# Block numbers loaded singly, and k + e and v + e of a pair of steps in one instruction, in a graph transformer layer

## The chip, the cores and the metric

The kernel runs on one core of a Trainium2 chip. The metric is the device time of one execution in microseconds (us); of several executions the median counts. The engines are PE (TensorE), DVE (VectorE), ACT (ScalarE), POOL (GpSimd) and SP (SyncE, which only issues transfers). Each engine has a sequencer, which reads the instructions in order, waits for semaphores, handles registers and hands the work to the engine.

## The reference

One block of a graph network over 6250 nodes of 256 numbers and 106250 edges sorted by their target node: two graph attention layers (4 heads of 64), a linear attention over all nodes, and a mixture of 8 experts with top 2. All numbers are fp32. What the change touches is the edge part of a graph attention layer:

```python
q = (x @ Wq + bq).reshape(n, H, C); k = (x @ Wk + bk).reshape(n, H, C); v = (x @ Wv + bv).reshape(n, H, C)
e = (edge_attr @ We).reshape(-1, H, C)
kj = k[src] + e
vj = v[src] + e
logits = einsum('ehc,ehc->eh', q[dst], kj) / sqrt(C)
a = softmax of logits over the edges with the same dst
agg = segment_sum(vj * a[:, :, None], dst)
```

## The kernel before, in words

`build` runs one stage after the other: `plan`, `nodes` and `mix`, then for each of two layers `edges`, and after them `finish`, `route`, `dispatch`, `experts` and `combine`. The two `edges` stages are the long ones.

`edges` walks over 880 steps. A step is a tile of 128 edges together with the block of 128 target nodes that they go to; a tile that straddles two blocks makes two steps. `plan` writes two rows of numbers into `tab`, in partition 0 of SBUF: the tile of each step and, from column `z.NSP` on, its block. 20 steps (`T`) make a chunk, 10 (`HT`) a half, and there are 44 chunks. `chunks` writes out chunks 0 to 3, then runs a hardware loop of 20 iterations of two chunks (`p` is 0 in the first and 1 in the second), so 40 steps an iteration, and then writes out two more chunks that only finish lagging work. Every engine has such a loop of its own, and semaphores alone bring them into step.

For each step j of a chunk:

- SP loads the tile of edge attributes `ea`. POOL gathers k and v of the source nodes with an indirect transfer into `kv`, a ring of 10, and waits for `s_vj` before it fills a slot again.
- PE makes e = `ea` x `We` (L916, two halves, each in two passes) and q of the target nodes = `oht` x a block of `acc` (L919), both into `ps`, a ring of four PSUM banks. For L919 it needs the step's block number in a register. Then it makes `pa` (L938), the weighted sum of a step that lies 36 steps (`LAG`) back. L916 waits for `s_prod` of two pairs before, L938 for ACT's `w` and DVE's `s_acc`.
- DVE works on pairs of steps, `q` = 0 to 9 in a chunk, j = 2q. In a pair it adds `pa` of a lagging step into `acc` (L969, `add`), makes `kj` (L1016) and `vj` (L1028, a ring of 40 steps), adds the second lagging step (L969), multiplies `kj` by q (L1041) and reduces the product of the pair before (L977). Each `add` needs the block number of its lagging step in a register. Around the pairs stand a one-hot matrix for 10 steps (L961, twice a chunk) and short chains of small instructions for the maximum and its rescaling, at q = 2 to 5 and 8. Most of these small ones wait on `s_m` for the one before.
- ACT scales `vj` by the exponentials into `w` (L897, L899).

Block numbers go into registers through `table` (L102), which is one TENSOR_LOAD of the sequencer for up to 10 numbers. Before the change PE loads 10 at the start of each half, ahead of L916. DVE loads in an iteration 6 numbers at q = 0 of the first chunk, 10 at q = 3, 10 at q = 8 (its last ones are kept for the second chunk), and in the second chunk 10 at q = 3 and 4 at q = 8: five loads, 40 numbers.

Of the kernel before, what the change touches and what calls it, by code (L numbers as in the profile page):

```python
# [23 lines left out]
P = 128  # L24
D = 256
# [719 lines left out]
def edges(nc, z, g, layer, a):  # L745
# [3 lines left out]
    with Stage(nc, f"edge{layer}") as st:  # L749
# [7 lines left out]
        kj = st.sb("kj", [P, 2, 2, D])  # L757
        vj = st.sb("vj", [P, RV, D])
# [29 lines left out]
        s_we, s_np, s_far, s_oht, s_ix, s_step, s_spare, s_pe, s_kj, s_vj, s_prod, s_red = (  # L788
            st.sem(n) for n in ("s_we", "s_np", "s_far", "s_oht", "s_ix", "s_step", "s_spare", "s_pe", "s_kj", "s_vj", "s_prod", "s_red"))
# [16 lines left out]
        def main(c):  # L806
            return not isinstance(c, int) or c < NCH
# [95 lines left out]
        def _(pe):  # L903
# [3 lines left out]
            def chunk(c, p, u, kept):  # L907
                for j in range(T):
                    s = c * T + j
                    if main(c):  # L910
                        if j % HT == 0:
                            blocks = table(nc, pe, g.tab[0:1, bass.ds(z.NSP + s, HT)], z.NB - 1)
                        pe.wait_ge(s_ea[j % HT], 32 * c + 16 * (j // HT) + 16)
                        need(pe, s_prod, c * HT + j // 2 - 1)
                        for k in range(2):
                            nc.tensor.matmul(ps[:, j % 4, 0:D], ea[:, j % HT, k, :], We[:, k, :], start=(k == 0), stop=(k == 1))  # L916
                        if j % HT == 0:
                            pe.wait_ge(s_oht, 2 * c + j // HT + 1)
                        nc.tensor.matmul(ps[:, j % 4, D:2 * D], oht[:, j // HT, (j % HT) * P:(j % HT + 1) * P],  # L919
                                         g.q[:, bass.ds(blocks[j % HT], 1), 0:D].rearrange("p o d -> p (o d)"), start=True, stop=True).then_inc(s_pe, 1)  # L920
# [21 lines left out]
        def _(dve):  # L942
# [28 lines left out]

            def reduce(c, p, q):
# [7 lines left out]
            def chunk(c, p, u, kept):  # L980
# [8 lines left out]
                for q in range(HT):  # L989
# [4 lines left out]
                    if q == 0 and here is None and lagged(c, 0):  # L994
                        here = [None] * 4 + list(table(nc, dve, g.tab[0:1, bass.ds(z.NSP + c * T - LAG, 6)], z.NB - 1))
# [3 lines left out]
                    if q == 3 and lagged(c, j):  # L999
                        here = table(nc, dve, g.tab[0:1, bass.ds(z.NSP + c * T + j - LAG, HT)], z.NB - 1)  # L1000
                    if q == 8 and lagged(c, j):
                        here = table(nc, dve, g.tab[0:1, bass.ds(z.NSP + c * T + j - LAG, HT if not p and not isinstance(c, int) else 4)], z.NB - 1)
# [5 lines left out]
                    if lagged(c, j):  # L1008
                        if q == 8:
                            dve.wait_ge(s_resc, c)  # L1010
                        add(c, j, here[(j + 4) % HT])
                    if main(c):
# [3 lines left out]
                        nc.vector.tensor_tensor(kj[:, q % 2, :, :], kv[:, both, 0:D], e, ALU.add).then_inc(s_kj, 1)  # L1016
# [9 lines left out]
                    if main(c):  # L1026
                        need(dve, s_w, c * T + j - (RV - 2))
# [695 lines left out]
```

## Time and profile before

| what | us |
|---|---|
| median of 3 runs | 5624.68 (5619.65 to 5625.87) |
| the profiled execution, its own time | 5591.4 |
| its span, first to last instruction | 5589.5 |
| edges of layer 1, from its first L919 to its last add | 480.2 to 2402.5 |
| edges of layer 2, likewise | 2650.0 to 4593.3 |

The profile describes one execution. Its own time is 1.8 us more than its span, and 33 us (0.6%) under the median of the runs shown, so a difference found in the profile is taken off the median. The mean granted TensorE clock is 0.911; within the two loops of `edges` it is 0.95 and 0.96.

### The profile page before, as it was taken

The page shows a single profiled execution, that of the slowest core. Times are in us where ns is not written, and L with a number is a line of the kernel's source. Part 1 is how long each engine was busy: PE and PEld are TensorE (multiplying, and loading weights), DVE is VectorE, ACT ScalarE, POOL GpSimd, SP SyncE. Part 2 cuts the span into 40 slices and gives each one's busy share as a digit, 9 for nine tenths or more (in the row PEclk, how much of TensorE's full clock was granted, in tenths as well). Part 3 has the DMA queues.
Part 4 walks back from the last instruction along what each step waited for, and adds up shares of the span by engine and source line. Part 5 has one row for each costly group of instructions (what it writes and reads, how often), then busy time and mean ns, then how long its engine had stood idle before and what let it go on. Part 6 is the DMA issues. An engine that isn't in the chain of part 4 may idle for free. (4 is left out here: it accounts for less than half of the span.)

```text
span 5589.5 us, 99514 instructions
## 1 busy us (share of the span) xinstructions
PE 4402.2 (79%) x18414; PEld 3403.3 (61%) x18415; DVE 4000.3 (72%) x8475; ACT 2763.5 (49%) x10075; POOL 2149.0 (38%) x2298
## 2 busy tenths in 40 slices
PE   3977988888888888878988888888888873139980
PEld 1546777777777777633777777777777752126650
DVE  4446988888888888854988888888888877302222
ACT  0122666666666666631566666666666661013320
POOL 1013544444444444300544444444444424430005
PEclk9999999999999999989999999999999985569995
DMA  4468666666666666534866666666666633432225
GB/s 94 135 217 243 187 182 187 185 181 186 182 191 189 180 187 182 150 112 148 235 185 185 182 181 188 182 183 183 179 186 180 186 102 101 173 97 64 64 78 153
DMA packets 617069, 919.99 MB, mean 165 GB/s; under 512 B 114486, under 2 KB 478582, under 8 KB 616535
## 3 DMA queue, kind: packets, MB, share of 16 engines
q0 software_dynamic: 154544, 502.26, 31.6%
q1 hardware_dynamic: 378966, 326.18, 20.9%
q10 hardware_dynamic: 83280, 89.03, 4.6%
q14 instruction: 251, 2.05, 0.1%
q8 instruction: 28, 0.46, 0.0%
HBM read 803.82 MB, written 113.31 MB: 164 GB/s over the span
## 5 line engine op out<-in xcount | busy, mean ns | idle before, releaser
L859 POOL DMA_INDIRECT edge_kv<-kvD,edge_ix x1760 | 1812.2, 1030 | 1914.7 <-DVE edge_vj L1028 1612.1
L897 ACT ACTIVATE edge_w<-edge_vj,edge_ex 128x64 f32<-128x64 f32 x7040 | 1864.8, 337 | 1012.4 <-PE edge_pa L938 903.6
L916 PE MATMUL edge_ps<-edge_We,edge_ea 112*128 112x256 f32 x7040 | 1906.6, 394 | 201.2 <-issue 173.9
L916 PEld LDWEIGHTS edge_ps<-edge_We,edge_ea 112*128 112x128 f32 x7040 | 1363.4, 196 | 495.5 <-issue 252.8
L938 PE MATMUL edge_pa<-edge_w,edge_oh 128*128 128x260 f32 x3520 | 1143.9, 409 | 309.2 <-DVE acc L969 298.9
L969 DVE SCALAR_TENSOR_TENSOR acc<-acc,flag,edge_pa 128x260 f32 x1760 | 839.2, 477 | 411.8 <-issue 320.7
L919 PE MATMUL edge_ps<-acc,edge_oht 128*128 x3520 | 1089.7, 391 | 0.0
L938 PEld LDWEIGHTS edge_pa<-edge_w,edge_oh 128*128 128x128 f32 x3520 | 647.7, 198 | 523.5 <-issue 322.4
L919 PEld LDWEIGHTS edge_ps<-acc,edge_oht 128*128 128x128 f32 x3520 | 697.8, 198 | 104.5
L1016 DVE TENSOR_TENSOR edge_kj<-edge_kv,edge_ps 128x512 f32<-128x512 f32 x880 | 600.0, 682 | 118.0 <-PE edge_ps L919 114.6
L1041 DVE TENSOR_TENSOR edge_prod<-edge_kj,edge_ps 128x512 f32<-128x512 f32 x880 | 598.6, 680 | 0.0
L1028 DVE TENSOR_TENSOR edge_vj<-edge_kv,edge_ps 128x512 f32<-128x512 f32 x880 | 597.3, 679 | 0.0
L977 DVE TENSOR_REDUCE edge_Lc<-edge_prod 128x8 f32<-128x512 f32 x880 | 597.2, 679 | 0.0
L470 PE MATMUL nodes_pj<-nodes_W,nodes_xT 128*128 128x512 f32 x784 | 361.7, 606 | 28.1 <-ACT nodes_xT L411 28.1
L899 ACT ACTIVATE edge_w<-edge_ex 128x4 f32<-128x4 f32 x1760 | 343.2, 195 | 0.0
L872 ACT ACTIVATE edge_oht<-edge_kb,edge_npart 128x1280 f32<-128x1280 uint8 x178 | 239.9, 1348 | 198.6 <-POOLq L858 101.4
L1544 DVE TENSOR_TENSOR exp_hb<-exp_pH,b 128x512 f32<-128x512 f32 x108 | 74.7, 692 | 325.9 <-PE exp_pH L1487 325.9
L961 DVE TENSOR_TENSOR edge_oh<-free,relS 128x1280 f32<-128x1280 f32 x176 | 260.8, 1482 | 0.0
L470 PEld LDWEIGHTS nodes_pj<-nodes_W,nodes_xT 128*128 128x128 f32 x784 | 144.3, 194 | 182.5 <-issue 146.0
L874 ACT ACTIVATE edge_oht<-edge_oht,ones 128x1280 f32<-128x1280 f32 x178 | 242.5, 1362 | 5.8
L542 DVE TENSOR_TENSOR acc<-nodes_pj,nodes_bias 128x256 f32 (+1 forms) x98 | 41.6, 425 | 236.2 <-PE nodes_pj L470 236.2
L1487 PE MATMUL exp_pH<-W,exp_xT 128*128 x432 | 205.3, 598 | 0.1
(230 smaller groups left out, 2878.6 us busy)
## 6 DMA issues: line engine op xcount, KB each, us to landing
edge_ea<-ea_t_dram SPq DMA_DIRECT2D x1760, 112.0 KB, 3.5
edge_kb<-relD SPq DMA_DIRECT2D x178, 160.0 KB
edge_kv<-kvD,edge_ix POOLq DMA_INDIRECT x1760, 4.4
kvD<-nodes_kvs ACTq DMA_DIRECT2D x98, 256.0 KB
xsD<-mix_zr POOLq DMA_DIRECT2D x27, 512.0 KB
exp_xr<-xsD SPq DMA_DIRECT2D x108, 128.0 KB, 2.1
ysD<-exp_yo ACTq DMA_DIRECT2D x108, 128.0 KB, 1.7
edge_pen<-penD SPq DMA_DIRECT2D x352, 32.0 KB
```

Of the source, the lines that this page charges most:

```text
L470: ins = nc.tensor.matmul(pj[:, j % 2, n * 2 * D:(n + 1) * 2 * D], xT[:, j, c, :], W[:, c, n * 2 * D:(n + 1) * 2 * D], start=(c == 0), stop ...
L859: nc.gpsimd.indirect_dma_start(out=kv[:, j % HT, :], out_offset=None, in_=g.kvD, in_offset=bass.IndirectOffsetOnAxis(ap=ix[:, h, j % HT:j ...
L897: nc.scalar.activation(w[:, j % 4, h * CA:h * CA + C], vj[:, slot, h * C:(h + 1) * C], ACT.Copy, scale=ex[:, x, h, k:k + 1])
L899: nc.scalar.activation(w[:, j % 4, :].rearrange("p (h k) -> p h k", h=H)[:, :, C], ex[:, x, :, k], ACT.Copy).then_inc(s_w, 1)
L916: nc.tensor.matmul(ps[:, j % 4, 0:D], ea[:, j % HT, k, :], We[:, k, :], start=(k == 0), stop=(k == 1))
L919: nc.tensor.matmul(ps[:, j % 4, D:2 * D], oht[:, j // HT, (j % HT) * P:(j % HT + 1) * P], g.q[:, bass.ds(blocks[j % HT], 1), 0:D].rearrang ...
L938: nc.tensor.matmul(pa[:, j % 2, 0:A], oh[:, par, (j + 4) % HT, :], w[:, j % 4, :], start=True, stop=True).then_inc(s_ape, 1)
L969: nc.vector.scalar_tensor_tensor(out=at, in0=at, scalar=g.flag[:, bass.ds(n, 1)], in1=pa[:, j % 2, 0:A], op0=ALU.mult, op1=ALU.add).then_i ...
L977: nc.vector.tensor_reduce(Lc[:, p, :, s:s + 2].rearrange("p h s -> p s h"), prod[:, q % 2, :, :].rearrange("p s (h k) -> p s h k", h=H), A ...
L1016: nc.vector.tensor_tensor(kj[:, q % 2, :, :], kv[:, both, 0:D], e, ALU.add).then_inc(s_kj, 1)
L1028: nc.vector.tensor_tensor(vj[:, p * T + j:p * T + j + 2, :], kv[:, both, D:2 * D], e, ALU.add).then_inc(s_vj, 1)
L1041: nc.vector.tensor_tensor(prod[:, q % 2, :, :], kj[:, q % 2, :, :], ps[:, bank, D:2 * D], ALU.mult).then_inc(s_prod, 1)
```

## The change

PE no longer loads ten block numbers before L916 of a half; it loads one number in every step, between L916 and L919. DVE no longer loads up to ten numbers at a time ahead of the first `add`; it loads two in every pair, for the pair that follows, behind the instruction that makes k + e and v + e and ahead of the second `add`. That instruction is new: `kj` and `vj` lie in one tile `kvj`, four rows for kj and forty for vj, and one TENSOR_TENSOR of 1024 elements a partition writes both, reading e twice through a stride of zero. The semaphore `s_kj` falls away and `s_vj` serves for both.

```diff
-        kj = st.sb("kj", [P, 2, 2, D])
-        vj = st.sb("vj", [P, RV, D])
+        kvj = st.sb("kvj", [P, 4 + RV, D])
+        vj = kvj[:, 4:4 + RV, :]
...
-                        if j % HT == 0:
-                            blocks = table(nc, pe, g.tab[0:1, bass.ds(z.NSP + s, HT)], z.NB - 1)
...
+                        block = table(nc, pe, g.tab[0:1, bass.ds(z.NSP + s, 1)], z.NB - 1)[0]
...
+            def both_of(row, slot):
+
+                at = kvj[:, row:row + 2, :]
+                part, pair, el = at.ap
+                return bass.AP(at.tensor, at.offset, [part, pair, [(4 + slot - row) * D, 2], el])
+
+            def blocks(n):
+                return table(nc, dve, g.tab[0:1, bass.ds(z.NSP + n, 2)], z.NB - 1)
...
-                    if q == 0 and here is None and lagged(c, 0):
-                        here = [None] * 4 + list(table(nc, dve, g.tab[0:1, bass.ds(z.NSP + c * T - LAG, 6)], z.NB - 1))
+                    if here is None and lagged(c, j):
+                        here = blocks(c * T + j - LAG)
...
-                    if q == 3 and lagged(c, j):
-                        here = table(nc, dve, g.tab[0:1, bass.ds(z.NSP + c * T + j - LAG, HT)], z.NB - 1)
...
-                        nc.vector.tensor_tensor(kj[:, q % 2, :, :], kv[:, both, 0:D], e, ALU.add).then_inc(s_kj, 1)
+                        need(dve, s_w, c * T + j - (RV - 2))
+                        nc.vector.tensor_tensor(both_of(2 * (q % 2), p * T + j), kv[:, both, :].rearrange("p t (b d) -> p t b d", b=2),
+                                                e.unsqueeze(2).to_broadcast([P, 2, 2, D]), ALU.add).then_inc(s_vj, 1)
...
-                    if main(c):
-                        need(dve, s_w, c * T + j - (RV - 2))
-                        nc.vector.tensor_tensor(vj[:, p * T + j:p * T + j + 2, :], kv[:, both, D:2 * D], e, ALU.add).then_inc(s_vj, 1)
                     if q == 5 and closed(c):
                         step(12)
                         nc.vector.tensor_scalar(Ym[:, :], mask4[:, :], dl[:, 0:1], None, ALU.mult).then_inc(s_Y, 1)
+                    if q == HT - 1 and (p or isinstance(c, int)):
+                        then = None
+                    elif lagged(c, j + 2):
+                        then = blocks(c * T + j + 2 - LAG)
+                    else:
+                        then = None
...
-                        add(c, j + 1, here[(j + 5) % HT])
+                        add(c, j + 1, here[1])
+                    here = then
```

**DVE at q = 3 of a chunk in the loop.** L102 ISA and TENSOR_LOAD are the register load; L969 (L968 in the changed file) is the add. Before:

```order
L998 STREAM_TRANSPOSE edge_TT<-edge_FB 128x32
L102 ISA
L102 TENSOR_LOAD tab
L966 REGISTER_ALU
L969 ISA
L969 SCALAR_TENSOR_TENSOR acc<-acc,flag,edge_pa 128x260
L1015 REGISTER_ALU
L1016 TENSOR_TENSOR edge_kj<-edge_kv,edge_ps 128x512
L986 REGISTER_ALU
L1024 SCALAR_TENSOR_TENSOR edge_X<-edge_wp,edge_R,edge_TT 128x20
L1025 SCALAR_TENSOR_TENSOR edge_Y<-edge_wp,edge_TT 128x20
L1028 TENSOR_TENSOR edge_vj<-edge_kv,edge_ps 128x512
```

After the change the same place reads:

```order
L1006 STREAM_TRANSPOSE edge_TT<-edge_FB 128x32
L965 REGISTER_ALU
L968 ISA
L968 SCALAR_TENSOR_TENSOR acc<-acc,flag,edge_pa 128x260
L1019 REGISTER_ALU
L1021 TENSOR_TENSOR edge_kvj<-edge_kv,edge_ps 128x2x2x256
L994 REGISTER_ALU
L1030 SCALAR_TENSOR_TENSOR edge_X<-edge_wp,edge_R,edge_TT 128x20
L1031 SCALAR_TENSOR_TENSOR edge_Y<-edge_wp,edge_TT 128x20
L102 ISA
L102 TENSOR_LOAD tab
L994 REGISTER_ALU
```

The load has moved from between the transposition and the first add to behind the large instruction, and it is of two numbers. The copy of R (L1034, then L1043), which waits for both scans, follows the load, with no vj between it and the scans.

**DVE at q = 5.** Before, vj stood between dl (L1020) and Ym (L1031), which waits for dl. After the change:

```order
L1021 TENSOR_TENSOR edge_kvj<-edge_kv,edge_ps 128x2x2x256
L994 REGISTER_ALU
L1025 TENSOR_TENSOR edge_Df<-edge_pm,edge_B 128x128
L1026 SCALAR_TENSOR_TENSOR edge_dl<-edge_GX,edge_B 128x1
L994 REGISTER_ALU
L1034 TENSOR_SCALAR edge_Ym<-edge_mask,edge_dl 128x4
L102 ISA
L102 TENSOR_LOAD tab
L965 REGISTER_ALU
L968 ISA
L968 SCALAR_TENSOR_TENSOR acc<-acc,flag,edge_pa 128x260
```

Ym stands directly behind dl, and the register load directly behind Ym.

**PE, a step inside a half** (L916 is L914 in the changed file, L919 is L918, L938 is L937). Before:

```order
L916 MATMUL edge_ps<-edge_We,edge_ea 128x256 x2
L919 ISA
L919 MATMUL edge_ps<-acc,edge_oht 128x256
L935 REGISTER_ALU
L938 MATMUL edge_pa<-edge_w,edge_oh 128x260
```

After:

```order
L914 MATMUL edge_ps<-edge_We,edge_ea 128x256 x2
L102 ISA
L102 TENSOR_LOAD tab
L918 ISA
L918 MATMUL edge_ps<-acc,edge_oht 128x256
L934 REGISTER_ALU
L937 MATMUL edge_pa<-edge_w,edge_oh 128x260
```

A register load of one number stands in each step between the two kinds of matmul, and the load of ten at the head of a half is gone.

## Rows read from the trace of the kernel before

**Rows 1.** The page: busy time of each engine, share of the span, instructions.

```profile
PE 4402.2 (79%) x18414; PEld 3403.3 (61%) x18415; DVE 4000.3 (72%) x8475; ACT 2763.5 (49%) x10075; POOL 2149.0 (38%) x2298
```

**Rows 2.** DVE's loop branches: count, ns min/median/max, first and last start; layer 1, then 2.

```profile
L800 DVEq COMPARE_BRANCH  x20: 60/68/74, 708.6 to 2361.4; - x20
...
L800 DVEq COMPARE_BRANCH  x20: 55/63/74, 2880.3 to 4552.0; - x20
```

**Rows 3.** DVE's waits, 708.6 to 2361.4: us in total, times, longest.

```profile
DVE acc L969 <- issue: 134.8, 52, 3.1
DVE edge_kj L1016 <- PE edge_ps L919: 37.6, 63, 1.9
DVE acc L969 <- PE edge_pa L938: 26.0, 20, 2.4
```

**Rows 4.** DVE's timeline in pairs 0 to 2: start us, duration us.

```profile
1505.03 1.48 DVE L961 TENSOR_TENSOR edge_oh<-free,relS 128x1280 f32<-128x1280 f32 x1
1506.43 0.48 DVE L969 SCALAR_TENSOR_TENSOR acc<-acc,flag,edge_pa 128x260 f32 x1
...
1509.61 0.47 DVE L969 SCALAR_TENSOR_TENSOR acc<-acc,flag,edge_pa 128x260 f32 x1
1510.01 0.68 DVE L1016 TENSOR_TENSOR edge_kj<-edge_kv,edge_ps 128x512 f32<-128x512 f32 x1
1510.60 0.68 DVE L1028 TENSOR_TENSOR edge_vj<-edge_kv,edge_ps 128x512 f32<-128x512 f32 x1
1511.20 0.48 DVE L969 SCALAR_TENSOR_TENSOR acc<-acc,flag,edge_pa 128x260 f32 x1
```

**Rows 5.** DVE's timeline at q = 3 of the same chunk; idle time in brackets.

```profile
1513.54 0.21 DVE L998 STREAM_TRANSPOSE edge_TT<-edge_FB 128x32 f32<-128x32 f32 x1
1516.27 0.48 DVE L969 SCALAR_TENSOR_TENSOR acc<-acc,flag,edge_pa 128x260 f32 x1 [2.52 <-issue]
```

**Rows 6.** Register loads of one iteration, L102: ns min/median/max, start us.

```profile
L102 DVEq TENSOR_LOAD <-tab x1: 837/837/837, 1500.7 to 1500.7; - x1
...
L102 DVEq TENSOR_LOAD <-tab x1: 2291/2291/2291, 1513.7 to 1513.7; - x1
...
L102 DVEq TENSOR_LOAD <-tab x1: 1061/1061/1061, 1534.1 to 1534.1; - x1
...
L102 DVEq TENSOR_LOAD <-tab x1: 349/349/349, 1575.9 to 1575.9; - x1
...
L102 PEldq TENSOR_LOAD <-tab x1: 2402/2402/2402, 1519.1 to 1519.1; - x1
```

**Rows 7.** DVE's timeline around the load at q = 8.

```profile
1533.31 0.68 DVE L1016 TENSOR_TENSOR edge_kj<-edge_kv,edge_ps 128x512 f32<-128x512 f32 x1
...
1536.10 0.42 DVE L1007 TENSOR_TENSOR acc<-acc,edge_fn 128x260 f32 x1
```

**Rows 8.** PE's register loads in `experts`, one number each.

```profile
L1471 PEldq TENSOR_LOAD <-etab x216: 297/302/546, 4977.7 to 5420.3; - x108
```

**Rows 9.** DVE around a loop branch: sequencer's records, then its timeline.

```profile
L800 DVEq COMPARE_BRANCH  x1: 68/68/68, 1497.1 to 1497.1; - x1
L800 DVEq FUSED_REGOPS  x1: 98/98/98, 1500.5 to 1500.5; - x1
...
1501.85 0.48 DVE L969 SCALAR_TENSOR_TENSOR acc<-acc,flag,edge_pa 128x260 f32 x1 [2.70 <-issue]
```

**Rows 10.** dl and Ym with nothing between them, behind the loop.

```profile
2378.08 0.21 DVE L1020 SCALAR_TENSOR_TENSOR edge_dl<-edge_GX,edge_B 128x1 f32<-128x1 f32 x1
2378.33 0.23 DVE L1031 TENSOR_SCALAR edge_Ym<-edge_mask,edge_dl 128x4 f32<-128x4 f32 x1
```

**Rows 11.** PE's timeline: two steps, and the one behind its load of ten.

```profile
1509.42 1.03 PE L916 MATMUL edge_ps<-edge_We,edge_ea 112*128 112x256 f32 x4
...
1511.16 1.03 PE L916 MATMUL edge_ps<-edge_We,edge_ea 112*128 112x256 f32 x4
...
1521.75 1.13 PE L916 MATMUL edge_ps<-edge_We,edge_ea 112*128 112x256 f32 x4 [1.12 <-issue]
```

More of the change, by code:

```diff
@@ L787, in edges @@
         s_pen = [st.sem(f"s_pen{h}") for h in range(2)]
-        s_we, s_np, s_far, s_oht, s_ix, s_step, s_spare, s_pe, s_kj, s_vj, s_prod, s_red = (
-            st.sem(n) for n in ("s_we", "s_np", "s_far", "s_oht", "s_ix", "s_step", "s_spare", "s_pe", "s_kj", "s_vj", "s_prod", "s_red"))
+        s_we, s_np, s_far, s_oht, s_ix, s_step, s_spare, s_pe, s_vj, s_prod, s_red = (
+            st.sem(n) for n in ("s_we", "s_np", "s_far", "s_oht", "s_ix", "s_step", "s_spare", "s_pe", "s_vj", "s_prod", "s_red"))
         s_oh, s_w, s_ape, s_acc, s_init = (st.sem(n) for n in ("s_oh", "s_w", "s_ape", "s_acc", "s_init"))
@@ L919, in chunk @@
                         nc.tensor.matmul(ps[:, j % 4, D:2 * D], oht[:, j // HT, (j % HT) * P:(j % HT + 1) * P],
-                                         g.q[:, bass.ds(blocks[j % HT], 1), 0:D].rearrange("p o d -> p (o d)"), start=True, stop=True).then_inc(s_pe, 1)
+                                         g.q[:, bass.ds(block, 1), 0:D].rearrange("p o d -> p (o d)"), start=True, stop=True).then_inc(s_pe, 1)
                     if closed(c):
@@ L998, in chunk @@
                         nc.vector.transpose(TT[:, :], FB[:, 112:144]).then_inc(s_m, 1)
-                    if q == 3 and lagged(c, j):
-                        here = table(nc, dve, g.tab[0:1, bass.ds(z.NSP + c * T + j - LAG, HT)], z.NB - 1)
-                    if q == 8 and lagged(c, j):
-                        here = table(nc, dve, g.tab[0:1, bass.ds(z.NSP + c * T + j - LAG, HT if not p and not isinstance(c, int) else 4)], z.NB - 1)
                     if q == 8 and closed(c):
@@ L1010, in chunk @@
                             dve.wait_ge(s_resc, c)
-                        add(c, j, here[(j + 4) % HT])
+                        add(c, j, here[0])
                     if main(c):
@@ L1037, in chunk @@
                     if lagged(c, j + 1):
[L1038 removed]
+                        add(c, j + 1, here[1])
+                    here = then
                     if main(c):
[L1040 to L1041 removed]
+                        dve.wait_ge(s_vj, c * HT + q + 1)
+                        nc.vector.tensor_tensor(prod[:, q % 2, :, :], kvj[:, 2 * (q % 2):2 * (q % 2) + 2, :], ps[:, bank, D:2 * D], ALU.mult).then_inc(s_prod, 1)
                     if q == 4 and closed(c):
```

2 lines of the change are left out of this document (removed).

## The prediction

> **What bounds the kernel now.** I read the page first. PE has the larger busy share, 79% to DVE's 72% [rows 1], which says little, since other stages are in it. The loops of `edges` are where the change acts, so I took DVE's loop branches next: 19 intervals in 1652.8 us of layer 1 and in 1671.7 us of layer 2 [rows 2], 87.0 and 88.0 us an iteration of 40 steps. 40 iterations at 87.5 are 3500 us of 5589.
>
> In them PE repeats a step every 1.74 us where nothing holds it (1509.42 to 1511.16 [rows 11]), 69.6 us for 40 steps, about 71.5 with the small matmuls. That leaves it 16 us of slack. DVE has less. Its waits in layer 1 [rows 3], divided by 19, are 7.1 us for "issue", 2.0 us for PE's L919 and 1.4 us for PE's L938, some 10.5 in all; the remaining 76.5 it works. So DVE sets the pace, and what shortens DVE's own stream or its stalls comes off the time, until 71.5 is reached.
>
> An issue stall is DVE's sequencer reading registers. At q = 3 the transposition starts at 1513.54 and the next add at 1516.27, 2.52 us idle [rows 5], and the load of ten lasts from 1513.7 for 2.29 us [rows 6]. At q = 8 a load of ten begins at 1534.1 [rows 6], just when kj, which the product before it waits for, has ended (1533.31 + 0.68), and L1007 starts at 1536.10 with no idle time [rows 7]. The sequencer had handed out four instructions and loaded beneath them. So a load costs nothing where work is queued ahead of it, and everything where the sequencer has just waited for DVE's newest result.
>
> **Cost of a load.** The durations [rows 6] are 2.29 us for ten numbers at q = 3, 1.06 for ten at q = 8, 0.84 for six, 0.35 for four; PE takes 2.40 for ten, and 0.30 for a single one [rows 8]. The fast ones start at a column divisible by four (20c - 20, 20c - 36), the slow ones two beyond (20c - 30, 20c + 10). It fits that four aligned numbers are read at once and all others singly, at 0.30 for the first and 0.22 to 0.24 for each further. A load of two is then 0.30 + 0.24 = 0.54 us; the bounds are 0.30 (read together) and 0.84 (the load of six).
>
> **The change part by part, for an iteration.**
>
> Removed: the two stalls at q = 3, 2 x 2.52 = 5.0 us. The loads at q = 8 were hidden, so nothing comes back there.
>
> Merged: kj and vj start 0.59 and 0.60 us apart from what follows, 1.19 us for both, and 1280 elements take 1.40 (1505.03 to 1506.43) [rows 4]. From 512 to 1280 elements that is 1.05 ns an element, so 1024 take 1.13 us: 0.06 less a pair, 1.2 us for 20 pairs. L961 reads both inputs by broadcast and keeps that rate, so I take the same for a zero stride; it reads no PSUM, and the other bound is no gain at all, 0.0.
>
> The Trainium skill ("VectorE: DVE Perf Modes", section on the TRN2 errata) puts a fixed 120 cycles on each PSUM source instruction, 125 ns. By it the merge would give 2.5 us an iteration instead of 1.2, and the sum would be about 50 us lower. The trace's 0.595 us for 512 elements leaves only 0.06 us of fixed part, and I go by the trace.
>
> PE's loads: the stall of 1.12 us at 1521.75 [rows 11] is the rest of its load of 2.40. The load of one (0.30), its address (0.05) and the way from a load's end to a started matmul (1521.5 to 1521.75, 0.25) make 0.60 us a step. Above them lie the four passes of L916 just handed out, 1.03 us [rows 11]. I cost them at nothing; without the cover they would be 24 us an iteration. Of DVE's 2.0 us of waits for L919, which follow PE's stalls, I take 1.5 as gone.
>
> The Trainium skill ("DMA: Bandwidth & Descriptors", section "Latency and other measured facts") gives a register load a floor of about 600 ns, to be spread by unrolling, which speaks against loading singly. By it PE's chain would be 0.90 us, still under 1.03, and the forecast would move by some 5 us only. The 216 single loads at 0.302 us contradict it.
>
> DVE's loads in an ordinary pair: the sequencer passes the product's wait when the large instruction ends, hands out product and reduction, waits for the add before (done about 0.1 us later), hands out the next add and the next large instruction, and loads for 0.6 us. The engine needs 0.40 + 0.60 + 0.60 + 0.40 + 1.13 = 3.1 us for what is queued. Cost nothing; uncovered it would be 0.85 us, as follows.
>
> Added at q = 5: Ym must wait for dl with nothing between, 0.25 us from start to start [rows 10] where 0.13 is usual for so small an instruction, so 0.12. Then the load starts about 0.16 after Ym (1513.54 to 1513.7 at q = 3), lasts 0.54, and the add starts 0.27 after its end (1516.0 to 1516.27). These 0.97 less Ym's own 0.22 are 0.75. Together 0.9, twice an iteration 1.8 us.
>
> Added at q = 3: the copy of R directly behind the scans, about 0.1, twice 0.2 us. The load there lies beneath the large instruction, handed out just before.
>
> The loop branch: DVE's sequencer takes 3.4 us from branch to first instruction (1497.1 to 1500.5), then loads six numbers, and 2.70 us show as idle [rows 9]. Queued above it were vj, add, product and reduction. After the change vj is not among them (0.6 us less cover), and the load is 0.3 us shorter: 0.3 us more.
>
> Sum: -5.0 - 1.2 - 1.5 + 1.8 + 0.2 + 0.3 = -5.4 us an iteration, -216 us for 40. The four written-out chunks with both kinds of work (2 and 3 in each layer) lose about 2.6 each, -10; in chunks 0 and 1, which PE limits, some of its eight load stalls go, an estimate of -9. Total -235 us. The profiled execution's 5591.4 becomes 5356; the median of 5624.68, from which I take the same difference, 5390.
>
> **The rivals.**
>
> *Part of the gain is missing.* The merged instruction saves nothing (+48 us), or PE, which needs 3.48 us a pair against DVE's 3.1, holds DVE up in the stretches with no extra DVE work, so that its 2.0 us of waits stay (+60). For it: 63 waits on L919, 0.6 us in the mean, stand in 19 iterations now [rows 3]. Against: the one-hot's 1.40 us and the chains give PE its lead back twice a chunk. Both together make 5498; one of them 5440 to 5450.
>
> *More is gained.* Waits for L938 and the longer issue stalls (up to 3.1 us [rows 3]) shrink as well since PE no longer stands: up to 2 us more an iteration, 5310.
>
> *Slower: PE's single loads are not hidden.* The place is between L916 and L919 in each step. If PE's sequencer cannot reach the load while L916 runs, 0.60 us a step turn 71.5 into 95.5 us an iteration, 8 above today: 40 x 8 = +320, about 5945. It decides when more than 16 / 40 = 0.40 us a step is exposed. Against it: PE's load of ten began at 1519.1 and cost only 1.12 us of idle, so it ran beneath matmuls [rows 6, 11].
>
> *DVE's loads are not hidden.* 18 pairs an iteration at 0.85 us would be 15 us more, a net +10, and 6015; it would be slower than before from 0.30 us a load. The hidden load of ten at q = 8 speaks against it. So does the one of four.
>
> *No change.* DVE's gains are eaten by another wait, such as ACT's or the gathers'. POOL is busy for 38% and ACT for 49% [rows 1], so I find none.
>
> **How the numbers follow.** The forecast's case, 5340 to 5430, has 0.67. Part of the gain missing (5430 to 5530) has 0.16, more gained (under 5340) 0.07, no change 0.03, slower by either way 0.07. The range of 8 in 10 runs from 5335 to 5480; it holds either of the smaller losses but not both. 0.2% of the time, 11 us, is about what a measurement of this kernel tells from no change. Faster 0.90, same 0.03, slower 0.07.
>
> **What would show it.** The interval of DVE's branches falls from 87.0 and 88.0 to about 82. L102 on DVE shows 0.54 us for two numbers, on PE 0.30 for one. The idle 2.52 us before L969 at q = 3 is gone, and about 0.75 appears before the second add at q = 5. The large instruction's duration is 1.22 us, and the next starts 1.13 after it. PE shows no idle time between L914 and L918. The prediction is wrong if the ordinary pair takes over 3.2 us, if PE's step exceeds 2.0 us, or if idle time appears before adds in every pair.

## The result, and the profile after

The changed kernel takes 5324.68 us in the median of 4 runs (5321.81 to 5326.23), the kernel before 5625.27 in the 4 runs beside it: a ratio of 0.9458, 95% interval 0.9432 to 0.9484. That is 300 us less, where 235 were forecast, and 10 us below the range. The profiled execution took 5325.0 us, its span 5322.8.

The page, to be held against [rows 1]: busy time of each engine.

```profile
PE 4324.0 (81%) x18414; PEld 3332.1 (63%) x18415; DVE 3957.8 (74%) x7595; ACT 2772.1 (52%) x10075; POOL 2076.2 (39%) x2298
```

DVE's loop branches in layer 1 and layer 2, as [rows 2]:

```profile
L800 DVEq COMPARE_BRANCH  x20: 55/63/74, 710.1 to 2242.8; - x20
...
L800 DVEq COMPARE_BRANCH  x20: 55/63/74, 2762.1 to 4292.4; - x20
```

Nineteen intervals each: 80.67 and 80.54 us for 40 steps, where [rows 2] gave 87.0 and 88.0. So the loops give 6.3 and 7.4 us an iteration, and the forecast said 5.4.

The waits of DVE between the first and last of those branches of layer 1, as [rows 3] (us in total, times, the longest):

```profile
DVE acc L968 <- issue: 89.0, 57, 3.8
DVE acc L968 <- DVE acc L1011: 11.4, 38, 0.3
DVE edge_kvj L1021 <- PE edge_ps L918: 2.2, 1, 2.2
...
DVE acc L968 <- PE edge_pa L937: 0.2, 1, 0.2
```

The two waits for PE, 63 and 20 times in [rows 3], have come down to one each. "Issue" falls from 134.8 us to 89.0; its 57 times are three an iteration, the two at q = 5 and the branch. The wait behind L1011 (L1007 before), 11.4 us, is the same in the kernel before. Layer 2, between its first and last of those branches, first before (2880.3 to 4552.0), then after (2762.1 to 4292.4):

```profile
DVE acc L969 <- issue: 161.9, 57, 3.8
DVE edge_kj L1016 <- PE edge_ps L919: 41.5, 64, 1.9
DVE acc L969 <- PE edge_pa L938: 13.9, 18, 1.7
```

```profile
DVE acc L968 <- issue: 86.2, 57, 3.6
...
DVE edge_kvj L1021 <- PE edge_ps L918: 2.9, 2, 2.3
```

The register loads (ns min/median/max), as [rows 6, 8]:

```profile
L102 PEldq TENSOR_LOAD <-tab x1760: 295/302/494, 480.5 to 4288.4; - x196
...
L102 DVEq TENSOR_LOAD <-tab x880: 522/528/778, 545.9 to 4326.4; - x176
```

DVE in order of time (start, duration, idle time before it). An iteration's q = 5, with an ordinary pair behind it, as [rows 4]:

```profile
1502.26 0.21 DVE L1026 SCALAR_TENSOR_TENSOR edge_dl<-edge_GX,edge_B 128x1 f32<-128x1 f32 x1
1502.51 0.23 DVE L1034 TENSOR_SCALAR edge_Ym<-edge_mask,edge_dl 128x4 f32<-128x4 f32 x1
1503.48 0.48 DVE L968 SCALAR_TENSOR_TENSOR acc<-acc,flag,edge_pa 128x260 f32 x1 [0.74 <-issue]
...
1506.87 1.21 DVE L1021 TENSOR_TENSOR edge_kvj<-edge_kv,edge_ps 128x1024 f32<-128x1024 f32 x1
1508.00 0.48 DVE L968 SCALAR_TENSOR_TENSOR acc<-acc,flag,edge_pa 128x260 f32 x1
...
1509.98 1.22 DVE L1021 TENSOR_TENSOR edge_kvj<-edge_kv,edge_ps 128x1024 f32<-128x1024 f32 x1
```

The large instruction holds the engine for 1.13 us (1506.87 to 1508.00), the pair lasts 3.11 (to the next large one at 1509.98). The load of two stands under the large instruction and the add, and nothing is idle. At q = 5 nothing is queued above the load but small instructions: 0.74 us. The loop branch and q = 3, as [rows 9, 5]:

```profile
1522.80 0.49 DVE L968 SCALAR_TENSOR_TENSOR acc<-acc,flag,edge_pa 128x260 f32 x1 [3.07 <-issue]
...
1534.31 0.21 DVE L1006 STREAM_TRANSPOSE edge_TT<-edge_FB 128x32 f32<-128x32 f32 x1
1534.61 0.48 DVE L968 SCALAR_TENSOR_TENSOR acc<-acc,flag,edge_pa 128x260 f32 x1
```

The 2.52 us of q = 3 are gone. The branch shows 3.07 instead of 2.70.

### The profile page after: what moved, and what is told of

It is laid out like the page before. It is cut to its first block and busy times, and to the rows that moved or that the text cites. A ratio compares the mean times of both kernels' runs of the same rounds, so it can differ in the third digit from the quotient of the medians.

```text
span 5322.8 us, 103674 instructions
## 1 busy us (share of the span) xinstructions
PE 4324.0 (81%) x18414; PEld 3332.1 (63%) x18415; DVE 3957.8 (74%) x7595; ACT 2772.1 (52%) x10075; POOL 2076.2 (39%) x2298
## 5 line engine op out<-in xcount | busy, mean ns | idle before, releaser
L859 POOL DMA_INDIRECT edge_kv<-kvD,edge_ix x1760 | 1737.6, 987 | 1726.0 <-DVE edge_kvj L1021 1152.7
L897 ACT ACTIVATE edge_w<-edge_kvj,edge_ex 128x64 f32<-128x64 f32 x7040 | 1865.3, 337 | 838.4 <-PE edge_pa L937 576.2
L914 PE MATMUL edge_ps<-edge_We,edge_ea 112*128 112x256 f32 x7040 | 1855.1, 386 | 45.0 <-DVE edge_prod L1051 23.2
L914 PEld LDWEIGHTS edge_ps<-edge_We,edge_ea 112*128 112x128 f32 x7040 | 1334.3, 192 | 291.7 <-issue 88.7
L937 PE MATMUL edge_pa<-edge_w,edge_oh 128*128 128x260 f32 x3520 | 1119.1, 401 | 281.8 <-DVE acc L968 174.9
L1021 DVE TENSOR_TENSOR edge_kvj<-edge_kv,edge_ps 128x1024 f32<-128x1024 f32 x880 | 1068.6, 1214 | 58.5 <-PE edge_ps L918 28.7
L918 PE MATMUL edge_ps<-acc,edge_oht 128*128 x3520 | 1063.5, 383 | 0.0
L968 DVE SCALAR_TENSOR_TENSOR acc<-acc,flag,edge_pa 128x260 f32 x1760 | 842.0, 478 | 235.8 <-issue 180.6
L937 PEld LDWEIGHTS edge_pa<-edge_w,edge_oh 128*128 128x128 f32 x3520 | 615.2, 191 | 534.1 <-ACT edge_w L899 249.6
L918 PEld LDWEIGHTS edge_ps<-acc,edge_oht 128*128 128x128 f32 x3520 | 679.9, 193 | 96.8
L1051 DVE TENSOR_TENSOR edge_prod<-edge_kvj,edge_ps 128x512 f32<-128x512 f32 x880 | 599.1, 681 | 1.1
L1515 PE MATMUL exp_pY<-W,exp_hT 128*128 x864 | 204.3, 379 | 0.0
```

The lines of the kernel that those rows point to most:

```text
L859: nc.gpsimd.indirect_dma_start(out=kv[:, j % HT, :], out_offset=None, in_=g.kvD, in_offset=bass.IndirectOffsetOnAxis(ap=ix[:, h, j % HT:j ...
L897: nc.scalar.activation(w[:, j % 4, h * CA:h * CA + C], vj[:, slot, h * C:(h + 1) * C], ACT.Copy, scale=ex[:, x, h, k:k + 1])
L937: nc.tensor.matmul(pa[:, j % 2, 0:A], oh[:, par, (j + 4) % HT, :], w[:, j % 4, :], start=True, stop=True).then_inc(s_ape, 1)
L968: nc.vector.scalar_tensor_tensor(out=at, in0=at, scalar=g.flag[:, bass.ds(n, 1)], in1=pa[:, j % 2, 0:A], op0=ALU.mult, op1=ALU.add).then_i ...
L1021: nc.vector.tensor_tensor(both_of(2 * (q % 2), p * T + j), kv[:, both, :].rearrange("p t (b d) -> p t b d", b=2), e.unsqueeze(2).to_broadc ...
L1051: nc.vector.tensor_tensor(prod[:, q % 2, :, :], kvj[:, 2 * (q % 2):2 * (q % 2) + 2, :], ps[:, bank, D:2 * D], ALU.mult).then_inc(s_prod, 1)
```

## The experiments

Medians of two kernels that were not run side by side are compared by their ratio to the kernel before, which ran beside each. Interval means DVE's loop interval, nineteen of them in each layer (nine of 80 steps, halved, in the last three rows with the long loop).

| kernel | median us | ratio, 95% interval | interval in layer 1, 2 |
|---|---|---|---|
| e1 before again | 5617.6 | 1.0005 (0.9985 to 1.0024) | 87.9, 87.5 |
| e2 merge only | 5652.1 | 1.0072 (1.0049 to 1.0095) | 87.8, 88.6 |
| e3 DVE's loads only | 5467.9 | 0.9741 (0.9719 to 0.9763) | 84.1, 83.5 |
| e4 PE's loads only | 5482.4 | 0.9769 (0.9747 to 0.9791) | 83.8, 85.0 |
| e5 both loads, no merge | 5259.8 | 0.9390 (0.9363 to 0.9417) | 79.5, 79.5 |
| e6 merge and DVE's loads | 5512.4 | 0.9847 (0.9821 to 0.9873) | 85.7, 85.5 |
| the change, all three | 5324.7 | 0.9458 (0.9432 to 0.9484) | 80.7, 80.5 |
| e7 the change, loads at the large instruction | 5224.5 | 0.9330 (0.9303 to 0.9357) | 79.0, 78.9 |
| e8 before, aligned loads | 5331.9 | 0.9512 (0.9485 to 0.9540) | 80.6, 81.4 |
| e9 the change, q = 5 load moved | 5233.0 | 0.9337 (0.9312 to 0.9363) | 79.1, 79.1 |
| e10 the change, four chunks a loop | 5318.3 | 0.9496 (0.9469 to 0.9522) | 79.7, 82.3 |
| e11 e7, four chunks a loop | 5258.9 | 0.9381 (0.9355 to 0.9407) | 78.3, 81.2 |
| e12 e7, four chunks for DVE alone | 5189.8 | 0.9260 (0.9242 to 0.9277) | 77.6, 77.7 |

**e1: the kernel before, unchanged.** 

> The kernel before, unchanged, for a second trace of it. The profiled execution of before was 5591, its medians 5625, while the changed kernel's executions all lie within 5 us. Theory 1 (the offset is real and sits in the loops): this trace shows a loop interval of DVE above 87.5 us in both layers, the 3.4 us from branch to first instruction nearer to the 4.0 that layer 2 had, and a time near 5625. Theory 2 (the first profile was an odd one in other stages): the loop intervals are again 87.0 and 88.0, and the difference lies outside the loops.

The profiled execution of before had been 33 us under its medians; this one has a span of 5625.1. Its loops differ from those of the first trace by +17 us in layer 1 and -9 in layer 2; the rest, 28 us, lies outside the loops: 13 ahead of the first branch of layer 1 and 14 between the two layers' loops. So the trace of before that the prediction used was a short one (the 12 executions here lie between 5589 and 5636), and mostly outside the loops. DVE's waits over its nineteen iterations of layer 1 (722.0 to 2392.1):

```profile
DVE acc L969 <- issue: 148.9, 89, 3.0
DVE edge_kj L1016 <- PE edge_ps L919: 43.0, 53, 2.0
DVE acc L969 <- PE edge_pa L938: 29.8, 22, 2.4
```

**e2: the merged instruction alone,** block numbers loaded as before.

```diff
-                        nc.vector.tensor_tensor(kj[:, q % 2, :, :], kv[:, both, 0:D], e, ALU.add).then_inc(s_kj, 1)
+                        nc.vector.tensor_tensor(both_of(2 * (q % 2), p * T + j), kv[:, both, :].rearrange("p t (b d) -> p t b d", b=2),
+                                                e.unsqueeze(2).to_broadcast([P, 2, 2, D]), ALU.add).then_inc(s_vj, 1)
...
-                        nc.vector.tensor_tensor(vj[:, p * T + j:p * T + j + 2, :], kv[:, both, D:2 * D], e, ALU.add).then_inc(s_vj, 1)
```

> Before, with k + e and v + e in one instruction and all register loads as before. My theory (sizes as predicted): 0.06 us a pair saved, 1.2 us an iteration, against 0.4 for Ym and R directly behind what they wait for and up to 0.6 less cover at the loop branch: -0.2 us an iteration, about 5615, not clearly different from before. Rival (the merge carries a good part of the 300 us): 1.2 us or more an iteration, 5570 or less.

It made the kernel slower, by 0.5 to 1.0%, where no clear difference was expected. Its waits in 710 to 2240:

```profile
DVE acc L969 <- issue: 152.0, 60, 3.8
DVE edge_kvj L1023 <- PE edge_ps L919: 30.9, 28, 2.2
DVE acc L969 <- PE edge_pa L938: 12.3, 13, 1.7
DVE edge_kvj L1023 <- issue: 11.0, 23, 0.7
```

In e1 the same stretch has 136.6 us of issue before L969 and 2.4 before L1016, and 39.9 and 29.8 of waits for PE. So 24 us more of sequencer time show here, in 17.4 iterations, which fits that vj no longer stands as cover between a load or a branch and the add; 26 us less of waits for PE go against it, as a DVE that is late waits less. What the merge saves is spent on that, and in layer 2, whose interval is 1.1 us longer than e1's, more than that.

**e3: DVE's loads alone,** two numbers in every pair, PE and the two instructions as before.

```diff
-                        here = table(nc, dve, g.tab[0:1, bass.ds(z.NSP + c * T + j - LAG, HT)], z.NB - 1)
...
+                        then = blocks(c * T + j + 2 - LAG)
```

> Before, with DVE's block numbers loaded in pairs, kj and vj apart, PE loading ten as before. My theory: the two idle stretches of 2.5 us at q = 3 go, little comes at q = 5 since vj stands before Ym, and 0.3 goes at the branch: -5.3 us an iteration, about 5400. Rival (PE's load of ten then becomes what holds the pairs, since both engines stall near each other): PE waits rise above 3 us an iteration and the time stays above 5450.

```profile
DVE acc L969 <- PE edge_pa L938: 50.8, 48, 2.3
DVE edge_kj L1015 <- PE edge_ps L919: 43.4, 43, 1.9
DVE acc L969 <- issue: 34.0, 37, 2.4
```

In 710 to 2240, 18.2 iterations: issue before the add has fallen from 7.8 us an iteration to 1.9, but the waits for PE stand at 5.2 (e1: 4.0 in the same stretch). A DVE that stalls less waits for PE more, and the interval falls by 3.9 instead of 6. So the rival of the expectation came true, with waits above 3 us and a time over 5450.

**e4: PE's single loads alone.**

```diff
-                        if j % HT == 0:
-                            blocks = table(nc, pe, g.tab[0:1, bass.ds(z.NSP + s, HT)], z.NB - 1)
...
+                        block = table(nc, pe, g.tab[0:1, bass.ds(z.NSP + s, 1)], z.NB - 1)[0]
```

> Before, with PE's block number loaded singly and DVE as before. My theory: the waits of DVE for L919, 2.0 us an iteration, go almost wholly: -1.5 to -2.5 us, 5525 to 5565. Rival 1 (single loads are exposed on PE): slower than before. Rival 2 (the waits for L919 come from elsewhere): no change, 5615 to 5625.

```profile
DVE acc L968 <- issue: 142.6, 66, 2.9
...
DVE edge_kj L1015 <- PE edge_ps L918: 2.6, 4, 2.0
```

This is the run that decides. With nothing changed but PE's loads, 69.7 us of waits for PE (39.9 for L919 and 29.8 for L938 in e1's 710 to 2240) are 2.6, and L938's do not appear at all. In layer 2 (e1 2924.7 to 4587.0, e4 2824.6 to 4439.2) 47.7 us are 9.0. The interval falls by 4.1 us in layer 1 and 2.5 in layer 2, 3.3 in the mean where 1.5 to 2.5 were expected, and the time by 2.3%.

TensorE's clock is a rival that this run bears on. In the trace of before the clock fell for a few microseconds twice in the iteration of [rows 4], each time behind some 2.5 us in which PE had waited for DVE's add: the granted clock was 0.60 in 1517 to 1521 and 0.72 in 1557 to 1561, so most of the first stretch ran at the lower of its two levels (1.2 and 2.4 GHz). A PE at half speed could have made DVE wait just as well. But e4's clock is hardly higher (0.97 in 710 to 2190 and 0.96 in 2770 to 4190, where e1 has 0.95 and 0.96), and DVE hardly waits for PE. So these stretches alone do not hold DVE up; how much they add to a stall of PE's load, no run shows.

**e5: both kinds of load, kj and vj apart.** 

> The changed kernel without the merge: DVE loads in pairs, PE singly, kj and vj apart. Theory 1 (the merge's 1.2 us an iteration is paid back, since with kj and vj apart nothing stands exposed at q = 5 and 0.6 us more work covers the loop branch): DVE idle about 3 us an iteration, interval about 79, 5260 to 5300, faster than the changed kernel. Theory 2 (the merge brings its 1.2 us once the loads are right): 5365 to 5380.

DVE's waits over its nineteen iterations of layer 1 (697.7 to 2208.6), and the three of one iteration in order of time, two at q = 5 and the one behind the branch:

```profile
DVE acc L968 <- issue: 59.1, 57, 3.0
```

```profile
1520.14 0.48 DVE L968 SCALAR_TENSOR_TENSOR acc<-acc,flag,edge_pa 128x260 f32 x1 [0.29 <-issue]
1558.94 0.48 DVE L968 SCALAR_TENSOR_TENSOR acc<-acc,flag,edge_pa 128x260 f32 x1 [0.63 <-issue]
1577.66 0.48 DVE L968 SCALAR_TENSOR_TENSOR acc<-acc,flag,edge_pa 128x260 f32 x1 [2.21 <-issue]
```

No wait for PE is left. It is faster than the whole change: 0.7% by the ratios, 38 us, and 1.1 us an iteration, 44 us, by the loops. (By the medians it is 65, but the kernel before ran 23 us shorter beside e5 to e8 than beside the changed kernel.) vj still stands between dl and Ym, and that shortens the idle time at q = 5 without taking it away: 0.29 and 0.63 us where the changed kernel has 0.74 twice. Behind the branch it is 2.21 where the changed kernel has 3.07. Together 3.1 us an iteration are idle here and 4.7 there. Apart, e3 and e4 gave 147 and 133 us, 280 together; here it is 343, so DVE's gain by its own loads is paid out in full only when PE is not late.

**e6: the merge with DVE's loads, PE as before.** 

> The changed kernel with PE's loads of ten as before. Theory 1 (PE's loads of ten hold DVE up by 3.9 us an iteration whatever DVE does): 5460 to 5480. Theory 2 (PE's part matters only beside DVE's own stalls, which are gone here): 60 us or less above the changed kernel, 5385 or less.

```profile
DVE acc L969 <- PE edge_pa L938: 72.1, 68, 1.8
DVE acc L969 <- issue: 50.6, 17, 3.5
DVE edge_kvj L1022 <- PE edge_ps L919: 47.4, 54, 1.9
```

119.5 us of waits for PE in 17.9 iterations, 6.7 each: the most of all kernels. The time, 5512, is above both theories'. Without PE's part the other two are worth 90 us of 300.

**e7: the change, with DVE's load of two directly behind the large instruction,** ahead of the chains, in every pair.

```diff
                                                 e.unsqueeze(2).to_broadcast([P, 2, 2, D]), ALU.add).then_inc(s_vj, 1)
+                    if q == HT - 1 and (p or isinstance(c, int)):
+                        then = None
+                    elif lagged(c, j + 2):
+                        then = blocks(c * T + j + 2 - LAG)
+                    else:
+                        then = None
                     if q == 5 and closed(c):
```

> The changed kernel with the pair's register load directly behind the large instruction at every q, so ahead of Df, dl and Ym at q = 5. If the 0.74 us of idle at q = 5 are the load alone: idle gone, 1.5 us an iteration, 60 us, about 5265. Rival (Ym's wait for dl is the stall, wherever the load stands): 5315 to 5325.

```profile
1468.99 0.23 DVE L1040 TENSOR_SCALAR edge_Ym<-edge_mask,edge_dl 128x4 f32<-128x4 f32 x1
1469.28 0.48 DVE L968 SCALAR_TENSOR_TENSOR acc<-acc,flag,edge_pa 128x260 f32 x1
```

The 0.74 us before the add at q = 5 are gone, twice an iteration, and the interval falls by 1.6 to 1.7: 66 us for 40. By the ratios (0.9330 against 0.9458) the gain is 72 us. The two profiled spans differ by 99; the other 33 lie outside the loops (the first branch stands at 694.9 instead of 710.1, and 495.0 us lie between the layers' loops instead of 519.3), of the size by which two executions of the kernel before differ there, too (e1). But e9 has most of it again (697.3 and 501.2), so it need not be spread; its cause is open. Against e5, the kernel without the merge, this one is 0.5 us an iteration faster. That does not show the merge to be worth anything: e5 still has its load behind vj and Ym and 0.9 us of idle time at q = 5 in layer 1, 0.6 in layer 2. An estimate from these numbers puts e5 with its load moved at 79.5 - 0.9 = 78.6 and 79.5 - 0.6 = 78.9 us, no slower than the 79.0 and 78.9 here; no run tried it.

**e8: the kernel before with its loads of ten made loads of twelve that start two numbers earlier,** at a column divisible by four. PE's loads of ten at the head of a chunk (j = 0) already start at such a column; they keep their start and are made twelve long. Only the loads change; the two extra numbers are not used.

```diff
-                            blocks = table(nc, pe, g.tab[0:1, bass.ds(z.NSP + s, HT)], z.NB - 1)
+                            blocks = table(nc, pe, g.tab[0:1, bass.ds(z.NSP + s - (2 if j else 0), HT + 2)], z.NB - 1)[(2 if j else 0):]
...
-                        here = table(nc, dve, g.tab[0:1, bass.ds(z.NSP + c * T + j - LAG, HT)], z.NB - 1)
+                        here = table(nc, dve, g.tab[0:1, bass.ds(z.NSP + c * T + j - LAG - 2, HT + 2)], z.NB - 1)[2:]
```

> The kernel before, with the two kinds of slow loads starting two numbers earlier, at a column divisible by four, and reading twelve numbers of which the first two are left unused. If four aligned numbers are read at once: 0.8 us instead of 2.3 to 2.4 on DVE and PE, idle time at q = 3 falls by 1.5 us and the waits for PE by most of 4, together 5 to 6 us an iteration, 5380 to 5430. If each number costs 0.23 wherever it lies: 2.8 us a load, and about 5640.

Its loads in 1400 to 1600, and the stall at q = 3:

```profile
L102 DVEq TENSOR_LOAD <-tab x13: 352/853/1074, 1401.4 to 1591.3; - x13
...
L102 PEldq TENSOR_LOAD <-tab x10: 846/850/854, 1405.5 to 1586.3; - x10
```

```profile
1524.76 0.48 DVE L969 SCALAR_TENSOR_TENSOR acc<-acc,flag,edge_pa 128x260 f32 x1 [1.08 <-issue]
```

Twelve numbers in 0.85 us where ten took 2.29 and 2.40 (and 1.09 on PE at j = 0). The stall falls from 2.52 to 1.08, DVE has no wait for PE left in 710 to 2240, and the old kernel with its loads aligned has 90% of the change's gain (0.9512 against 0.9458). The time is 48 us below the expected range.

**e9: the change, with only the load of q = 5 moved** behind the large instruction.

```diff
+                    if q == 5:
+                        then = blocks(c * T + j + 2 - LAG) if lagged(c, j + 2) else None
```

> The changed kernel with one load moved: at q = 5 alone DVE's two numbers are loaded directly behind the large instruction, before the chain of dl and Ym; at every other q the load stays where the change put it. In e7, where all were moved, the loops gained 1.6 us an iteration (64 us for 40) and the stretches outside the loops another 35 to 40. Theory 1: the uncovered load at q = 5 is the whole of what the loops gained, two of 0.74 us an iteration: loop interval about 79.0 us, and 60 us less than the changed kernel, about 5265. The gain outside the loops then does not come with it (or, if it does, the same uncovered load also stretched the written-out chunks: then 5225). Theory 2: the place of the load matters in every pair, since behind the large instruction it is covered by more: then this kernel keeps part of the 80.6 us interval, 79.8 or more, and comes out over 5290.

In 775 to 2195, 18 iterations, DVE's issue waits are 55.6 us in 18 times, one an iteration, that of the branch. The loop intervals are e7's within 0.12 us and the ratio lies within e7's interval: in the loops the load at q = 5 was all of it, and in the other pairs its place does not matter. The time is 32 us under the 5265 of the theory, by what lies outside the loops (e7).

**e10: the change, with the hardware loop written out for four chunks,** 10 iterations of 80 steps.

```diff
-            with eng.Fori(2, NCH // 2) as i:
-                kept = chunk(2 * i, 0, i, None)
-                chunk(2 * i + 1, 1, i, kept)
+            with eng.Fori(1, NCH // 4) as i:
+                for k in range(2):
+                    kept = chunk(4 * i + 2 * k, 0, 2 * i + k, None)
+                    chunk(4 * i + 2 * k + 1, 1, 2 * i + k, kept)
```

> The changed kernel with the hardware loop written out for four chunks an iteration instead of two, so 10 iterations instead of 20 in a layer and 20 loop branches fewer in all on each engine. Theory 1: DVE's sequencer shows about 3.1 us idle before the first add behind each branch, and within an iteration the same place costs next to nothing, so 20 x 3 = 60 us go: about 5265. Theory 2: the time behind the branch is taken up by the slack of the other engines (PE waits in its turn for DVE, and its own branch lies in the same place), so half or less is gained, 5295 or more. Theory 3: the longer loop body costs instruction fetches elsewhere, no gain: 5320.

**e11: e7 with the same loop.** 

> The kernel of e7 (all of DVE's loads directly behind the large instruction) with the hardware loop of four chunks. If the two costs are separate, the gains add: 5224 less what e10 shows, 5165 if that is 60. If PE becomes the bound once DVE's idle time is gone (its step is 1.74 us where nothing holds it, 69.6 us for 40 steps and some 71.5 with the small matmuls, against an interval of 79 now), less is gained, but with 7 us of slack an iteration that is not expected: over 5200 would say so.

Neither paid: e10's interval of the ratio overlaps the change's, and e11 is 0.5% slower than e7 (e7's five executions lie between 5222 and 5234 us, e11's between 5251 and 5266). In layer 1 both loops are faster, by 1.0 and 0.7 us for 40 steps, in layer 2 slower, by 1.8 and 2.3. The branches in layer 2 (2700 to 4150; ns min/median/max), first e7's, then e11's:

```profile
L800 ACTq COMPARE_BRANCH  x18: 45/45/45, 2760.8 to 4102.6; - x18
L800 ACTq FUSED_REGOPS  x18: 59/59/59, 2761.0 to 4102.9; - x18
L800 PEldq COMPARE_BRANCH  x18: 207/208/208, 2766.8 to 4108.7; - x18
```

```profile
L800 ACTq COMPARE_BRANCH  x9: 45/45/45, 2758.9 to 4057.8; - x9
L800 ACTq FUSED_REGOPS  x9: 59/59/64, 2761.8 to 4060.3; - x9
L800 PEldq COMPARE_BRANCH  x9: 5206/5304/5620, 2765.0 to 4063.9; - x9
...
L800 DVEq COMPARE_BRANCH  x9: 63/63/74, 2767.6 to 4066.5; - x9
L800 DVEq FUSED_REGOPS  x9: 98/98/104, 2771.3 to 4070.4; - x9
```

From the branch to the instruction behind it (FUSED_REGOPS) ACT takes 0.2 us in the short loop and 2.5 to 2.9 in the long one; PE's branch itself takes 0.21 and 5.3 (3.8 in layer 1); DVE takes 3.7 to 3.9 in the long loop and 3.5 to 3.6 in e7's (its first here from 2769.4 to 2773.0). The transfers of instructions bear on what PE does there. e11's queue q8 of them in 2767.6 to 4229.5, nine iterations (transfers, MB, share of the DMA engines):

```profile
q8 instruction: 89, 1.46, 0.5%
```

In e7's eighteen iterations (2769.4 to 4190.3) and in e12, where DVE's loop alone is long, q8 carries nothing. PE in e11, behind such a branch:

```profile
3095.87 1.05 PE L915 MATMUL edge_ps<-edge_We,edge_ea 112*128 112x256 f32 x2 [5.01 <-issue]
3100.28 1.01 PE L915 MATMUL edge_ps<-edge_We,edge_ea 112*128 112x256 f32 x2 [3.35 <-issue]
...
3102.88 1.91 PE L915 MATMUL edge_ps<-edge_We,edge_ea 112*128 112x256 f32 x4
```

PE stands for 5.0 and 3.35 us, and DVE waits 77.4 us for L938 in 2770 to 4190, nine times (e7: none). Two of q8's transfers start right behind the branch (in 3090 to 3093) and a third, of 2.1 us, at 3096.7, where the second idle stretch begins. That fits a PE that waits there for its next instructions, but no run tests it. After the idle time PE's clock is at its lower level: the four passes of L915 take 1.91 us at a granted clock of 0.50 (3102.8 to 3104.8), where they take 1.03 at full clock. Over 2770 to 4190 the granted clock is 0.97 instead of e7's 0.99.

**e12: e7 with the loop of four chunks for DVE alone.**

```diff
+            if after == 3:
+                with eng.Fori(1, NCH // 4) as i:
...
+            else:
+                with eng.Fori(2, NCH // 2) as i:
...
-            chunks(dve, chunk)
+            chunks(dve, chunk, 3)
```

> The kernel of e7, with the loop of four chunks for DVE alone; PE, ACT, POOL and SP keep the loop of two. In e11, where all have the long loop, PE's COMPARE_BRANCH takes 3.7 us (layer 1) and 5.5 us (layer 2) instead of 0.21, and ACT's next instruction stands 2.6 us behind its branch instead of 0.2. Theory 1: those longer fetches of PE (two idle stretches of 5.0 and 3.35 us for each branch in layer 2) ate what DVE saved. With PE's loop short again DVE keeps 10 uncovered branches of about 3 us less in each layer: 77.4 to 77.7 us for 40 steps in both layers, 5160 to 5180. Theory 2: DVE's time behind a branch grows with its loop as PE's does (3.4 us in e7; 6 or more here), so that half as many cost as much: 5210 to 5230. Theory 3: DVE is held up by something else as soon as it runs faster, such as POOL's gathers: waits for L918 or for the transfer of kv appear, 5190 to 5220.

DVE's waits in 775 to 2160:

```profile
DVE acc L974 <- issue: 29.5, 9, 3.6
```

The intervals are theory 1's, 77.6 and 77.7 us, in both layers. The time is 10 us above theory 1's and at the edge of theory 3's, but none of theory 3's waits shows in layer 1, and 2.3 us of one for PE's L943 in layer 2 (2770 to 4150); the rest lies outside the loops again (581.1 us from layer 1's last branch to layer 2's first, at 2754.6; to the same step they are 573.9 in e7). It is the fastest kernel of the study, 7.4% under the kernel before and 2.1% under the changed one by their ratios.

## Why the prediction was wrong

The direction, the mechanism and the steps of DVE's own stream were right; one term of the sum was taken too small. The table sets the sum against the trace of before that it was made from and against e1's, over the loops of both layers (38 iterations), in us an iteration:

| term | predicted | before | after | after less before | after less e1 |
|---|---|---|---|---|---|
| sequencer idle (issue): q = 3 gone, q = 5 and branch added | -5.0 + 1.5 + 0.3 = -3.2 | 7.81 | 4.61 | -3.20 | -3.67 |
| waits for PE's L919 (after: L918) | -1.5 | 2.08 | 0.13 | -1.95 | -1.99 |
| waits for PE's L938 (after: L937) | 0 | 1.05 | 0.02 | -1.03 | -1.03 |
| add behind L1007 (after: L1011), q = 8 | 0 | 0.60 | 0.60 | 0 | +0.39 |
| work of DVE: merge, and the chain's gaps at q = 5 and 3 | -1.2 + 0.3 + 0.2 = -0.7 | | | -0.70, the rest | -0.79 |
| interval | -5.4 | 87.49 | 80.61 | -6.88 | -7.09 |

(e1's waits in layer 2, 2924.7 to 4587.0: 165.7 us of issue, 37.8 for L919, 9.9 for L938, 4.2 behind L1007; the last is 3.6 in layer 1.)

- **Waits for PE (the step that failed).** "Of DVE's 2.0 us of waits for L919, which follow PE's stalls, I take 1.5 as gone": all of them went, and so did L938's, which the sum left in. It was to be -3.0 and stood as -1.5. The 1.5 us missing are 60 us for 40 iterations, and the miss is 66 (300 us against 235); what is left is within what two executions differ by. e4 shows it without any change to DVE, and there the removal of PE's stalls is worth 3.3 us an iteration. In layer 1 alone the waits for L938 were larger (1.4 us, and 0.7 in layer 2).
- The error was to hold PE innocent because it had 16 us of slack an iteration. The slack is a mean. What the traces fit is that a stall of PE at the start of a half meets DVE at a place where PE has no lead, and nobody pays DVE back for a wait. The rival "more is gained" named this, at 5310, with a chance of 0.07 that was too low: nothing in [rows 3] spoke for L938's waits staying.
- **Cost of a load.** Predicted 0.54 us for two and 0.30 for one; measured 0.528 and 0.302. That the start of a load decides is confirmed by e8. But the rule as the prediction words it, four aligned numbers at once and all others singly, does not give the slow loads: ten numbers that start two beyond a multiple of four hold two aligned groups of four, and by it would take about as long as the 1.06 us of ten that start aligned. They took 2.29, as ten single ones would. What fits all the loads is that fours are counted from the start of the load and go at once only where that start is aligned; why is open. The Trainium skill ("DMA: Bandwidth & Descriptors", section "Latency and other measured facts") has a floor of about 600 ns for a register load; the trace does not agree, 1760 loads of PE have a median of 0.302 us.
- **q = 3, q = 5, the branch, the ordinary pair.** Predicted: 2.52 gone, 0.75 added before the second add, the branch 0.3 longer, no idle time in an ordinary pair of 3.1. Measured: gone, 0.74, 3.07 for 2.70, 3.11.
- **The merge.** Predicted 0.06 us less a pair; the engine is held for 1.13 us, as forecast, where two instructions took 1.19 [rows 4]. The term was right, but it was not the merge's whole effect: a part of the 1.8 us at q = 5 and the 0.3 at the branch, which the sum adds elsewhere, are also the merge's, since it takes vj away as cover (e5, with vj there, has 0.9 us of idle time at q = 5 and 0.9 less behind the branch). The sum had the pieces to say that the merge is a loss with the loads in this place, and did not say it. e5 against the change shows 38 us, e2 against e1 about 35.
- **The 125 ns rule.** The Trainium skill ("VectorE: DVE Perf Modes", section on the TRN2 errata) puts a fixed 120 cycles on each instruction that reads PSUM. One such instruction fewer a pair saved 0.06 us from start to start and not 0.125: as a saving of time the trace does not agree. The durations do: 0.68 us for 512 elements and 1.21 for 1024, where estimates by the page's formula are 0.66 and 1.19. But the next instruction starts 0.08 us before the end of the one ahead, and so only a part of the fixed cost counts.
- **PE's single loads hidden.** Right: PE's step stays at 1.74 us (L914 at 1507.61, 1509.35, 1511.08), and the rival that they show is out.
- **Outside the loops** -19 us were forecast. The spans of e1 and after differ by 302, the loops by 7.1 x 40 = 284 when the 38 intervals' mean stands for all 40, which leaves 18. From the trace of before the spans differ by 267, the loops by 6.9 x 40 = 275, and outside them after is 8 us longer. Two executions differ by more than this term, which stays unproven.

The forecast took the profile's difference off the median. From e1's trace the spans differ by 302 us, as the medians do (300); from the trace of before, which was short outside the loops, by 267. Its loops were no worse a source for the waits for PE than e1's: 3.1 us an iteration over both layers against 3.2.

## What to carry to other kernels

When an engine that is "not the bottleneck" stalls in bursts, count the bottleneck's waits for it, all of them, as the price of the bursts; slack in the mean does not hide them. Put a register load behind the largest instruction just handed out and ahead of any chain that waits for itself, and before fusing two instructions ask what the second one was covering. When a load of several numbers is slow, look at where it starts before making it smaller.

## What the runs showed of the hardware

**Register loads.** 0.302 us for one number and 0.528 for two; 0.35 for four, 1.06 to 1.09 for ten and 0.85 for twelve that start at a column divisible by four, but 2.29 to 2.40 for ten that start two beyond. Four aligned ones cost little more than a single one, and two take no less when their start is aligned: the 880 loads of two start now at a multiple of four, now two beyond, and half of them lie between 0.522 and 0.528 us.

**The branch of a loop costs by the length of its body.** The traces record between two branches 287 instructions of ACT in the short loop and 571 in the long one, 913 and 1823 of PE, 411 and 819 of DVE (e7, e11). The cost is 0.2 us for the short bodies of ACT and PE, and 2.5 us or more for the others. The queues of instruction transfers give a reason for PE: q8 carries nothing while PE's body is short and ten transfers an iteration, 162 KB, when it is long (e11). The Trainium skill ("Runtime: NRT & Kernel Launch", section "Instruction fetch mechanics") describes a store of 512 instructions (32 KiB), 2048 on PE (128 KiB), filled in blocks of 256, and says that a taken branch whose target is outside of the two blocks held waits for a fetch. By its size for PE the long body, 162 KB, does not fit and the short one, about half of it, does: the trace agrees. It agrees for ACT, whose 287 fit and 571 do not. DVE's 411 recorded instructions would fit, but q14 carries 93 transfers in e7's eighteen iterations, five of 8 KB in each or some 42 KB, and two of the five start within 7 us behind DVE's branch. That is over the 32 KiB that the page gives, so DVE's body seems to hold more than the trace records, if the five are DVE's. In e12, where DVE's loop alone is long, q14 carries 75 in nine iterations (2754.6 to 4152.9). The trace names the engine of neither queue, and no run made DVE's body shorter, so that DVE's cost has this cause is not shown.
